# The first expert matrix, 64 experts: two halves of 384 columns, 16 bytes apart, in its buffer

## The reference, cut to what matters

```python
x = x + 0.5 * _L0_ffn_ref(_layernorm(x), wg, shared_w1, shared_w2, expert_w1, expert_w2)
...
w_topk, idx_topk = jax.lax.top_k(softmax(x @ wg.T), 8)
buf = zeros((64, 160, 128)).at[expert, rank].set(x[token], mode='drop')
h = jnp.einsum('ech,efh->ecf', buf, expert_w1)          # expert_w1: 64 x 768 x 128
x1, x2 = jnp.split(h, 2, axis=-1)
out = jnp.einsum('ecf,ehf->ech', x1 * silu(x2), expert_w2)  # expert_w2: 64 x 128 x 384
combined = zeros((T, 128)).at[token].add(out * weight)
```

## Time and profile before

| what | us |
|---|---|
| median of 3 runs | 3281.98 |
| lowest, highest | 3276.39, 3284.52 |
| span of the profiled execution | 3607.6 |
| first stage of 64 units (355 to 592 of the span) | 237 |
| second stage of 64 units (1058 to 1294) | 236 |
| TensorE busy in the whole span | 2593.0 (72%) |
| GpSimd busy in the whole span | 1846.4 (51%) |

### The profile page before, as it was taken

The page is one execution under the profiler, slowest core; times in us unless marked ns, Lnnn a source line. Parts: engine busy times, 40 slices in busy tenths (PEclk is TensorE's granted clock), DMA queues, the critical chain, the costliest instruction groups (busy, mean ns, idle before and its releaser), DMA issues. The chain is left out here.

```text
span 3607.6 us, 68811 instructions
## 1 busy us (share of the span) xinstructions
PE 2593.0 (72%) x24634; PEld 1681.5 (47%) x24634; DVE 2038.9 (57%) x5864; ACT 1370.6 (38%) x2937; POOL 1846.4 (51%) x2072
## 2 busy tenths in 40 slices
PE   1224994735499945689998899947388886999573
PEld 1113884423368834356555555536133332555362
DVE  4347334523443345547885587621699999787413
ACT  1111221301122222344665266622576763466323
POOL 5650775254317742126996213456488886123554
PEclk7666997856599977799999799978699999899786
DMA  9100896121019974331110101112221211111123
GB/s 373 48 1 8 213 224 155 45 66 31 27 41 226 226 191 108 138 120 21 19 19 3 20 19 30 48 55 56 102 94 48 94 62 40 22 20 35 43 80 92
DMA packets 222721, 294.13 MB, mean 82 GB/s; under 512 B 36704, under 2 KB 179583, under 8 KB 216288
## 3 DMA queue, kind: packets, MB, share of 16 engines
q1 hardware_dynamic: 172704, 249.85, 22.3%
q0 software_dynamic: 47616, 39.44, 5.8%
q10 hardware_dynamic: 2112, 1.05, 0.1%
HBM read 181.88 MB, written 107.12 MB: 80 GB/s over the span
## 5 line engine op out<-in xcount | busy, mean ns | idle before, releaser
L3783 POOL TENSOR_TENSOR l3am_db<-l3am_du,l3am_bs 128x1024 f32<-128x1024 f32 x127 | 298.0, 2367 | 39.9 <-DVE l3am_hh L4021 36.1
L4021 DVE TENSOR_TENSOR_SCAN l3am_hh<-l3am_dA,l3am_db 128x1024 f32<-128x1024 f32 x128 | 292.1, 2283 | 0.9 <-ACT l3am_dA L3921 0.7
L1217 POOL TENSOR_TENSOR l2a_pT<-l2a_pT,kept 128x512 int32<-128x512 int32 x213 | 265.1, 1280 | 45.4 <-ACT l2a_pT L1423 45.4
L3066 POOL DMA_INDIRECT l0f_table<-l0f2e_y,l0f2e_idx x128 | 178.9, 1398 | 177.1 <-DVE l0f2e_idx L3038 130.2
L3066 POOL DMA_INDIRECT l0f_table<-l0f1e_y,l0f1e_idx x128 | 179.6, 1403 | 139.2 <-DVE l0f1e_idx L3038 91.2
L4152 PE MATMUL l3am_y<-l3am_hc,ident 128*128 128x512 f32 x512 | 242.1, 596 | 0.0
L3921 ACT ACTIVATE l3am_dA<-l3am_dl,l3am_al 128x512 f32<-128x512 f32 x256 | 166.3, 682 | 130.8 <-DVE l3am_hh L4021 127.2
L1894 POOL DMA_INDIRECT l0f_rows<-l0f1r_row,l0f1r_idx x160 | 159.7, 998 | 103.1 <-issue 69.3
L1304 DVE CUSTOM_DVE_ANT_0 l2a_junk<-l2a_s,addend 128x256 f32<-128x256 f32 x486 | 178.1, 421 | 57.0 <-PE l2a_s L1540 44.6
L1297 DVE TENSOR_REDUCE l3f1a_mx<-l3f1a_s 128x2 f32<-128x512 f32 x243 | 156.5, 685 | 40.9 <-PE l3f1a_s L1540 32.4
L1297 DVE TENSOR_REDUCE l3f2a_mx<-l3f2a_s 128x2 f32<-128x512 f32 x243 | 156.4, 684 | 39.7 <-PE l3f2a_s L1540 32.1
(11 more groups left out here) (848 smaller groups left out, 7045.5 us busy)
## 6 DMA issues: line engine op xcount, KB each, us to landing
l3am_bs<-l3a_b SPq DMA_DIRECT2D x32, 1024.0 KB, 6.6
l0f1m_w<-in_L_ffn_expert_w SPq DMA_DIRECT2D x64, 384.0 KB
l0f2m_w<-in_L_ffn_expert_w SPq DMA_DIRECT2D x64, 384.0 KB
l1a_top<-l1a_kernel SPq DMA_DIRECT2D x16, 1024.0 KB, 12.6
l0f_rows<-blank SPq DMA_DIRECT2D x8, 1930.0 KB, 15.2
l0f1m_w<-in_L_ffn_expert_w SPq DMA_DIRECT2D x64, 192.0 KB
l0f2m_w<-in_L_ffn_expert_w SPq DMA_DIRECT2D x64, 192.0 KB
l3f_rows<-blank SPq DMA_DIRECT2D x8, 1440.0 KB, 11.6
```

The source lines that it names most:

```text
L1217: self.nc.gpsimd.tensor_tensor(t, t, self.kept[:, f // 8 % 2, :].unsqueeze(1).to_broadcast([P, 2, 2 * P]), ALU.mult).then_inc(self.cut_g, 1)
L3066: g.indirect_dma_start(out=tables[p], out_offset=bass.IndirectOffsetOnAxis(ap=idx[u % RING][:, a:a + 1], axis=0), in_=y[u % RING][:, a, :] ...
L3783: G.tensor_tensor(db[n % DB][:, :].rearrange("p (j t) -> p j t", j=CC), du[k % 2][:, :, :], bs[s // QUARTER][:, s % QUARTER, :].unsqueeze( ...
L4021: V.tensor_tensor_scan(hh[n % HH][:, :], dA[n % 2][:, :], db[n % DB][:, :], 0.0, ALU.mult, ALU.add).then_inc(h_ready, 1)
```

## The change

The buffer of the first matrix becomes [128, 2, 388] in place of [128, 768] where there are 64 experts: two halves of 384 columns, each followed by 4 unused ones (16 bytes). The load's two sides are now 128 x 2 x 384, so it consists of 256 pieces of 1536 bytes instead of 128 of 3072. `first_of` gives the matmuls the slice for f = 0, 1, 2 in the first half and 3, 4, 5 in the second, which begins 1552 bytes into the partition. Everything allocated after the buffers moves by 4 x 32 bytes a partition at most.

```diff
         self.w1, self.w2, self.places = w1, w2, places
-        self.t1 = [ph.sb(f"w1_{i}", [P, C1 * P]) for i in range(places)]
+        self.parts, self.width = (2, C1 * P // 2) if C1 == 6 else (1, C1 * P)
+        pad = 4 if self.parts > 1 else 0
+        self.t1 = [ph.sb(f"w1_{i}", [P, self.parts, self.width + pad]) for i in range(places)]
...
     def load(self, sp, e, place):
-        sp.dma_start(self.t1[place][:, :], self.w1[bass.ds(e, 1), :, :].rearrange("a p f -> (a p) f")
+        sp.dma_start(self.t1[place][:, :, 0:self.width],
+                     self.w1[bass.ds(e, 1), :, :].rearrange("a p (h f) -> (a p) h f", h=self.parts)
                      ).then_inc(self.loaded[place], 16)
...
+    def first_of(self, t, f):
+        h, f = divmod(f * P, self.width)
+        return t[:, h, f:f + P]
...
-                    mm = nc.tensor.matmul(o, matrix(mats.t1, i, u)[:, f * P:(f + 1) * P], xeT[p][:, :], start=True, stop=True)
+                    mm = nc.tensor.matmul(o, mats.first_of(matrix(mats.t1, i, u), f), xeT[p][:, :], start=True, stop=True)
```

## The result

The changed kernel takes 3299.18 us, median of 9 runs (3291.64 to 3309.38); the kernel before takes 3281.98 us in the same measurement (3274.14 to 3295.49). The ratio is 1.0050, 95% interval 1.0036 to 1.0064: slower by 12 to 21 us. The forecast was 3285 with a range from 3264 to 3298, so the time lies outside the range, and it moved the way to which the forecast had given a chance of only 0.13 (slower by over 0.3%).

The account below looks back on a forecast made before the run. POOL was taken as the bound, TensorE's row loop hardly behind. Per stage, 3.8 us less most of the 2.6 us cushion plus 0.8 for landings gave +2.0; +3 was taken for two stages: 3285, range 3264 to 3298.

Parts of the forecast that it names:

- The bounds: In the two 64-unit stages, POOL within 10.4 us of its 217.5 us floor, TensorE hardly behind: 3.57 against 3.40 a unit.
- The cushion: POOL falls behind TensorE's y by 2.6 us over 64 units, taking up most of the load's added time per stage.
- The packets: First matrix's load: two 1536-byte packets take 132 ns against 124 for one of 3072, so 0.07 us more a matrix.
- rival C: First matrix's load: halves joined again into 3072-byte pieces on the way to the engines, nothing moves, 3282; chance 0.03.
- Its sentence on 0.03 us in place of 0.07: First matrix's packets: a skill page's overhead rule gives 0.03 us a matrix, not 0.07; result would move by under 2 us.
- The landings: POOL's waits for older adds to land: 12 a stage, each 0.07 us longer as loads share the engines, +0.8 us.
- The offset: Second halves beginning 1552 bytes into the partition: 0 to 0.07 us more a matrix, 0.01 taken.
- The issue: First matrix's issue on SyncE: 373 ns against 333, +0.04 us; later traffic start put at 0.04, between 0 and 0.06.
- The issues behind: Second matrix and rows on SyncE's queue: later issue costs nothing while the first matrix's traffic takes over a microsecond.
- Rival A: Queue of loads: long packets stall, short ones don't, up to 0.4 us a turn back; 3266, chance 0.13.
- Rival B: TensorE's row loop outruns POOL's distance behind y; at upper bounds a turn grows 0.23 us; 3294, chance 0.12.
- The remark on the profiler's 326 us: Profiled span 326 us above the median: if POOL's 0.30 us gaps are among them, its floor is lower without the profiler.

Follow-up runs that it names:

- Both kernels with rows first: Changed kernel and kernel before, each with the unit's rows issued ahead of its two matrices; ratios to before 0.9982 and 1.0016.
- the delays: Kernel before, 3072-byte pieces kept, with eight or five semaphore increments on SyncE between the two matrices' issues; ratios to before 1.0078 and 1.0062.
- the delay of eight: Kernel before with eight semaphore increments on SyncE between the two matrices' issues, rows issued 0.62 us later; ratio to before 1.0078.

## Why the prediction was wrong

- **The bounds, right.** POOL within 10 us of its floor and TensorE's row loop just behind. Both kernels with rows first show POOL's side (227 to 228 us with y 8 us ahead), the delays show the other.
- **The cushion, read too large.** It was put at 2.6 us a stage, from POOL's distance behind y at the start and at the very end. But the changed kernel, in which POOL doesn't fall behind inside the stage, ends at a distance of 2.2 us as well, since the last y wait for no loads. So 1.3 of the 2.6 us belong to the end of a stage, and what was used up is 3.46 - 2.16 = 1.3 us in the first stage and 3.85 - 2.14 = 1.7 in the second, together 3.0 and not 5.2. The time from first y to last grew by 10.1 and 7.8 us, and 17.9 - 3.0 is the 15 us of the stages. That 64 x 0.35 - 5.2 gives 17 as well is two errors that cancel: the rows don't land 0.35 us later but 0.27 and 0.25 (4.60 for 4.33 us behind y, 4.55 for 4.30), and half of that over 64 units of each stage is 17 us before the cushion. For the delay of eight that formula gives 34 where 25.5 came.
- **The packets, right.** 66 ns a packet was said and is there, and 45390 of the stretch's 45393 packets are under 2 KB, so the load did change and rival C fell. The whole price of the halving, with a short issue, is 0 to 6 us; within that, the 0.07 us a matrix was not resolved. (Its sentence on 0.03 us in place of 0.07 is a little low with "under 2 us": by its own sum, 0.08 us a turn are all within the cushion, 0.4 us a stage is left of 2.0, and the result moves by 3.)
- **The landings, wrong in sign.** The sum had 0.8 us a stage more of POOL's waits for landings. They fell, from 8.9 to 1.8 us in the first stage, while POOL's adds came further apart.
- **The offset, right.** Next to nothing was said, and with 64 bytes in place of 16 nothing changed.
- **The issue, wrong.** The step was "the nearest row with 256 pieces in two pieces a partition is the rows' load of the 8-expert stages, 373 ns [...] +0.04 us", with 0.06 as the bound. It measured +0.22 on the issue itself and +0.12 on the one behind. This is the term that made the forecast fail. The reading took the count of pieces as what the issue depends on. By the experiments it is the pair of address patterns: the nearest row was near in count only, its source steps don't join. That it was one row only, and no other split load was looked at, left the bound of 0.06 without ground.
- **The issues behind, wrong.** "The later issue of the second matrix and the rows lies beside the traffic of the first and costs nothing while that takes over a microsecond." The rows' last packet lands 3.03 us behind their issue before and 3.01 after (medians of 60 units in the first stage's packets): issued later, they land later by most of it. The cover wasn't one, and the two delay kernels price it. With 0.35 us in place of 0.04 the prediction's own sum has a turn grow by 0.43 us, a unit by 0.215, both stages by 27.5, less 5.2 and with 1.6 for landings: +24. That is outside its range on the right side and above the 17 that came, by the other terms named here.
- **Rival A**, that long packets stall, fell: it would have taken up to 0.4 us off the engines' time for a unit, and 2.34 became 2.32. The slices of after from 349 to 353 are as weak at a burst's start, 15 to 154 GB/s from 350.8 to 351.5, and first pass 300 at 351.9, with packets of half the length (in the earlier trace rows they pass 300 at 440.3, not at 440.2 as the prediction read):

```profile
DMA  9999999999999663209905283974899899999999
GB/s 369 399 384 338 399 392 400 308 283 301 249 206 149 105 87 62 26 0 92 92 15 108 46 154 138 276 200 184 266 312 312 261 307 333 276 287 302 328 353 369
```

- **Rival B** is what happened, by the sign that the prediction gave for it (a stage of over 240 us, POOL waiting for y and not for landings): the row loop outran the cushion and TensorE set the pace. It gave 3294 from three upper bounds met at once, when one mis-sized term was enough; 0.12 was too little because its weight hung on prices of packets and on the bound of 0.06 us for the issue.
- **The remark on the profiler's 326 us, wrong.** They aren't the profiler's: they go with where the trace was taken.

## What to carry to other kernels

Before a load is given another shape, look at what its issue costs on the queue, not only at its bytes and packets, and look for a load whose two address patterns relate as the new one's do. If other loads stand behind it in the same queue and someone waits for those, a longer issue is paid again in each round; here the cure for the loss was to put the load that is waited for first. Where one engine is at its floor and another just behind, speeding up the one behind gives nothing, while slowing it shows as soon as the distance between them is used up. Read that distance at the start and inside the stage, ahead of its last units, where nothing is waited for any more and the distance grows by itself.

## What the runs showed of the hardware

- SyncE takes 333 ns to issue a load of 128 pieces, 384 ns for 256 pieces in two per partition, and 556 ns for the same 256, or for 384 in three, when the source's steps join into one and the destination's don't. The next issue behind that one takes 450 instead of 333. That the joining is the cause fits all the forms tried (four long ones, two short ones of the same size, and the rows' loads); the sizes of the steps weren't varied on their own, and what SyncE does in that time is not seen in a trace.
- Halving packets from 3072 to 1536 bytes left the engines' time per unit where it was, within the 0.1 us or so by which it varies between these kernels: 2.34 us before, 2.32 after.
- A burst of loads after a lull ran at 15 to 184 GB/s for its first 0.7 to 0.8 us and passed 300 only after 1.0 to 1.1 us, with packets of 3072 bytes and of 1536 alike. It goes with standing first: in the kernel before, a packet of the first matrix takes 169 ns in the mean and one of the rows 42, and with the rows issued first 157 and 53 (first stage).
